# One tile's look-ahead and two ring slots fewer in a routed expert stage, and weight splitting moved from VectorE to GpSimd

## The reference

```python
def _moe(x, gate, w1, w2, w3):              # x: 4096 tokens of 256
    probs = softmax(xf @ gate)              # 4 experts
    w, idx = top_k(probs, 2); w = w / sum(w)
    comb = einsum('nk,nke->ne', w, one_hot(idx, 4))
    for e in range(4):
        h = silu(xf @ w1[e]) * (xf @ w3[e])           # 256 -> 768
        out = out + comb[:, e:e+1] * (h @ w2[e])      # 768 -> 256
...
x = x + _moe(_rmsnorm(x, g2), gate, w1, w2, w3)
...
x = x + s * silu(x_ffn)                     # the end of layer 1
```

## Time and profile before

| | |
|---|---|
| device time, median of 3 | 3390.69 us (3389.99 to 3396.9) |
| profiled execution | 3396.9 us, of which the span from first to last instruction is 3395.1 |
| busy in the span | TensorE 3159.0 us, VectorE 2242.8, ScalarE 2053.3, GpSimd 1165.1 |
| mean granted TensorE clock | 0.963 |
| routing stage | from 2769.4 to 2872.5 us |
| expert stage | from 2872.5 us to the end |

### The profile page before, as it was taken

How to read it: one execution, slowest core, us unless ns; L and a number is a source line. 1 busy time by engine, 2 the same in 40 slices (tenths; PEclk the granted TensorE clock), 3 DMA queues, 4 the chain that set the end, 5 groups by cost and what they waited for, 6 DMA issues and landing times. The chain is left out here.

```text
span 3395.1 us, 75760 instructions
## 1 busy us (share of the span) xinstructions
PE 3159.0 (93%) x23170; PEld 2407.6 (71%) x23170; DVE 2242.8 (66%) x6696; ACT 2053.3 (60%) x4941; POOL 1165.1 (34%) x1836
## 2 busy tenths in 40 slices
PE   4999999999999999999999988969999974999995
PEld 3777776777767767668888865546666664999995
DVE  5888888888888888876566655556666626333334
ACT  4777777777777777765655543226656644333433
POOL 4444444444444444443333320043242202333331
PEclk9999999999999999999999998969999976999998
DMA  3111111111111111143333431010111133223225
GB/s 87 34 36 36 33 28 31 36 36 36 36 32 36 36 36 36 32 144 125 131 111 129 136 124 50 32 49 25 34 44 33 33 107 113 35 39 88 37 37 169
DMA packets 143913, 208.80 MB, mean 62 GB/s; under 512 B 29762, under 2 KB 101826, under 8 KB 143778
## 3 DMA queue, kind: packets, MB, share of 16 engines
q1 hardware_dynamic: 130914, 189.46, 18.7%
q0 software_dynamic: 12864, 17.57, 3.2%
HBM read 123.22 MB, written 39.98 MB: 48 GB/s over the span
## 5 line engine op out<-in xcount | busy, mean ns | idle before, releaser
L770 POOL TENSOR_SCALAR at_p<-at_p,at_recip 128x512 f32<-128x512 f32 (+3 forms) x1030 | 538.1, 539 | 824.6 <-DVE at_recip L917 824.6
L826 ACT ACTIVATE at_p<-at_p,at_nmax 128x512 f32<-128x512 f32 (+3 forms) x1032 | 571.5, 556 | 130.4 <-DVE at_nmax L911 124.0
L911 DVE CUSTOM_DVE_ANT_0 at_p<-at_s_ps,at_bias 128x512 f32<-128x512 f32 (+3 forms) x1032 | 462.2, 488 | 63.3 <-PE at_s_ps L1043 44.7
L1889 DVE CUSTOM_DVE_ANT_0 aa_a_ps<-aa_a_ps,aa_hidden 128x128 f32<-128x128 f32 (+3 forms) x512 | 247.3, 507 | 177.1 <-PE aa_a_ps L2053 174.0
L1043 PE MATMUL at_s_ps<-at_k_twice,at_q 64*128 64x512 f32 (+3 forms) x3096 | 342.2, 340 | 3.1 <-DVE at_nmax L911 3.1
L1065 PE MATMUL at_o_ps<-at_pT,at_v 128*64 128x512 f32 (+3 forms) x2064 | 307.7, 440 | 0.0
L1789 ACT ACTIVATE aa_pT<-aa_b_ps 128x512 f32<-128x512 f32 (+1 forms) x384 | 196.7, 529 | 180.6 <-PE aa_b_ps L2071 177.9
L923 DVE COPY at_pT<-at_t_ps 128x512 f32<-128x512 f32 (+3 forms) x512 | 239.2, 488 | 94.0 <-PE at_t_ps L1055 90.2
L1055 PEld LDWEIGHTS at_t_ps<-ident,at_p 64*128 64x128 f32 x5120 | 189.2, 138 | 120.5 <-issue 120.5
L449 ACT ACTIVATE nw_h<-nw_h_ps,nw_b 128x512 f32<-128x512 f32 x192 | 132.3, 689 | 210.6 <-PE nw_h_ps L553 210.1
L526 DVE SCALAR_TENSOR_TENSOR nw_hl<-nw_h,nw_coef_now,nw_hh 128x512 fp32r<-128x512 f32 x192 | 150.2, 782 | 163.8 <-ACT nw_hh L454 163.8
(11 more groups left out here) (307 smaller groups left out, 7807.3 us busy)
## 6 DMA issues: line engine op xcount, KB each, us to landing
at_k_twice<-at_k_twice SPq DMA_DIRECT2D x130, 256.0 KB, 2.8
nw_w_raw<-in_w_all_dram SPq DMA_DIRECT2D x26, 1024.0 KB, 5.0
nw_w_raw<-in_w_all_dram SPq DMA_DIRECT2D x52, 512.0 KB, 6.8
w_all<-in_w_dram SPq DMA_DIRECT2D x12, 768.0 KB, 10.1
nw_xh<-xh_dram SPq DMA_DIRECT2D x10, 512.0 KB, 4.2
nw_xl<-xl_dram SPq DMA_DIRECT2D x10, 512.0 KB, 4.8
at_w_raw<-in_w_heads_dram SPq DMA_DIRECT2D x18, 256.0 KB, 3.7
nw_x<-in_x_dram SPq DMA_DIRECT2D x9, 512.0 KB, 6.0
```

What stands on the lines that cost most here:

```text
L770: pool.tensor_scalar(p, p, recip[:, u:u + 1], 1.0, ALU.mult, ALU.mult).then_inc(scaled, 1)
L826: act.activation(p_sb[:, u, 0:N], p_sb[:, u, 0:N], ACT.Exp, bias=nmax[:, u:u + 1], scale=-1.0, accum_out=total[:, u:u + 1]).then_inc(exped, 1)
L911: dve.tensor_tensor_reduce(out=p_sb[:, u, 0:N], in0=s_ps[u % 2][:, score_at(u // 2)], in1=bias[:, u % 2, S - N:S], scale=1.0, scalar=BIG, ...
L1889: dve.tensor_tensor_reduce(out=a_ps[i % 2][:, 0:N], in0=a_ps[i % 2][:, 0:N], in1=hidden[:, S - N:S], scale=1.0, scalar=BIG, op0=ALU.add, o ...
```

## The change

The expert stage keeps 3 buffers of gathered rows in place of 5, and turns the rows of tile t + 1 in unit 2t, right ahead of its hidden sums, in place of in unit 2t - 1; `take_x` and `rest_x` move with it. In routing the splitting during the votes is gone. ScalarE sums the squares of a batch before it copies the turned batch, and makes all 24 high parts behind the norms. GpSimd makes the 12 low parts of experts 2 and 3: six before the first part of the list, and two after each of the first three parts. VectorE makes those of experts 0 and 1 after `places`, as before.

```diff
-XRING = 5
+XRING = 3
...
-        SPLITS = [(e, piece) for e in (2, 3, 0, 1) for piece in W_PIECES]
-        SPLIT_BY = [0, 0, 0, 0, 2, 4, 6, 9, 12]
...
@@ routing_phase, gpsimd @@
+            def split_low(number, e, piece):
+                hi, lo = (slice(at, at + W_PIECE) for at in W_PIECES[piece])
+                pool.wait_ge(w_high, number + 1)
+                pool.tensor_tensor(w_all[:, e, lo], w_all[:, e, lo].bitcast(F32), w_all[:, e, hi].bitcast(F32), ALU.subtract)\
+                    .then_inc(w_low, 1)
+
             pool.memset(blank[:], 0.0).then_inc(blanked, 1)
             pool.wait_ge(loaded, 48)
+            pieces = [(e, piece) for e in (2, 3) for piece in range(len(W_PIECES))]
+            for number in range(6):
+                split_low(number, *pieces[number])
+
             for j in range(PARTS):
                 pool.wait_ge(marked, 2 * j + 2)
                 pool.tensor_tensor(told[j % 2][:, :, 0, :], in_tile[j % 2][:],
...
+                if j < PARTS - 1:
+                    for number in (6 + 2 * j, 7 + 2 * j):
+                        split_low(number, *pieces[number])
...
@@ routing_phase, scalar @@
             for b in range(B):
+                square(b)
                 copy_turned(b)
-                square(b)
-                for number in range(SPLIT_BY[b], SPLIT_BY[b + 1]):
-                    split_high(number)
...
             for b in range(2, B):
                 norm(b)
-            for number in range(SPLIT_BY[B], len(SPLITS)):
-                split_high(number)
+            for e in (2, 3, 0, 1):
+                act.wait_ge(w_loaded[e], 48)
+                for hi, lo in W_PIECES:
+                    act.activation(w_all[:, e, hi:hi + W_PIECE], w_all[:, e, lo:lo + W_PIECE].bitcast(F32), ACT.Copy)\
+                        .then_inc(w_high, 1)
...
@@ routing_phase, vector: in the votes @@
-                if b > 0:
-                    for number in range(SPLIT_BY[b - 1], SPLIT_BY[b]):
-                        split_low(number)
-            for number in range(SPLIT_BY[B - 1], SPLIT_BY[B]):
-                split_low(number)
...
@@ expert_phase, scalar (vector alike, with rest_x) @@
             take_x(0)
             pass_gate(0)
-            take_x(1)
...
-                if half == 1 and t + 2 < TILES:
-                    take_x(t + 2)
+                if half == 0 and t + 1 < TILES:
+                    take_x(t + 1)
...
@@ expert_phase, tensor @@
             turn_x(0)
             hidden_sums(0)
-            turn_x(1)
             hidden_sums(1)
             turn_hidden(0)
             for U in range(UNITS):
                 t, half = divmod(U, 2)
                 if half == 0 and t + 1 < TILES:
                     whose(t + 1)
-                if half == 1 and t + 2 < TILES:
-                    turn_x(t + 2)
+                    turn_x(t + 1)
                 if U + 2 < UNITS:
                     hidden_sums(U + 2)
```

More of the change, by code:

```diff
@@ L2383, in _ @@
             dve.wait_ge(loaded, 48)
[L2385 to L2389, removed]
             for k in range(KT):
@@ L2512, in _ @@
             dve.tensor_copy(shares[:], list_ps[:, LANES:2 * LANES]).then_inc(placed, 1)
-            for number in range(SPLIT_BY[B], len(SPLITS)):
-                split_low(number)
+            number = 2 * len(W_PIECES)
+            for e in (0, 1):
+                for hi, lo in (tuple(slice(at, at + W_PIECE) for at in piece) for piece in W_PIECES):
+                    number += 1
+                    dve.wait_ge(w_high, number)
+                    dve.tensor_tensor(w_all[:, e, lo], w_all[:, e, lo].bitcast(F32), w_all[:, e, hi].bitcast(F32), ALU.subtract)\
+                        .then_inc(w_low, 1)
         @block.tensor
@@ L2702, in _ @@
             gate(0)
-            rest_x(1)
             for U in range(UNITS):
@@ L2710, in _ @@
                     .then_inc(h_low, 1)
-                if half == 1 and t + 2 < TILES:
-                    rest_x(t + 2)
+                if half == 0 and t + 1 < TILES:
+                    rest_x(t + 1)
             for b in range(B):
```

## The result

The changed kernel takes 3609.13 us (median; 3603.01 to 3609.13, 3 runs) against 3390.69: the ratio is 1.0633, interval 1.0607 to 1.0658. It is slower, and lies beyond the forecast's range, which ended at 3600. Its profiled execution took 3604.48 us with a span of 3602.7, 207.6 more than the span of before; the mean granted clock went from 0.963 to 0.948. The forecast's sum was +159, and it is made against spans, so 48.6 us are to be explained.

What follows compares the result with a forecast made beforehand. The prediction took TensorE to bound the expert stage and VectorE's chain to set routing's end. Stall 141.2, ring +2, backlog -2 and routing +18 made +159 us: 3556 profiled, 3550 against the median, range 3512 to 3600.

Steps and rivals of the forecast that it cites:

- I take it that the clock holds, narrowly: Expert stage: TensorE keeps its full clock despite a pause of 2.16 us in 9.3.
- a clock of 0.5 in the expert stage: Expert stage: one of three signs in the profile after that would show the forecast wrong.
- Rival (b): Expert stage: the clock falls after some or all pauses, costing 33 to 88 us, 3583 to 3638; chance 0.17.
- The stall, 2.14 a tile: Expert stage: TensorE waits for the turned rows' round trip at half 0 of tiles 1 to 66, 141.2 us.
- Rival (d): Expert stage: shorter round trip, take_out and hh not in front, 1.60 a tile, 106 + 18: 3515; chance 0.08.
- The ring of three, +2: Expert stage: gathered rows come 0.8 late at the two places with side loads, with spill 2 us in all.
- Rival (f): Expert stage: ring too short throughout, each tile 0.8 longer if every gather took 7.3 us, +53: 3603; chance 0.03.
- The backlog at the tail, -2: End of expert stage: the last scatter's 2.91 us hold by earlier ones is gone with longer tiles, -2 us.
- Routing, +18: Routing stage: VectorE and GpSimd take turns; 5.4 before the first told, 10.7 between them, 2 for half clock.
- Rival (c): Routing stage: VectorE and GpSimd do not shut each other out, 141 - 3 = +138, 3529; chance 0.10.

Runs made afterwards that it cites:

- filler runs: Changed kernel with 1, 2, 3, 4 or 12 extra products of 128 columns, results unused, in the pause: 3603.84, 3606.03, 3606.42, 3556.95, 3556.40 us.
- e4: Changed kernel with take_x ahead of take_out and hh on ScalarE, and rest_x ahead of hl on VectorE: 3526.35 us, ratio 1.039.
- e3: Kernel before with only the changed routing stage, ring and order of the expert stage as before: 3405.49 us, ratio 1.0039.
- e7: Kernel with the routing part alone, but all 24 low parts on VectorE behind the list and none on GpSimd: 3400.81 us, ratio 1.0026.

## Why the prediction was wrong, by its own steps

- **"I take it that the clock holds, narrowly": this step failed.** The clock fell after 34 of the 66 pauses, at 1.56 us each, 53 us. The prediction had named a clock of 0.5 in the expert stage as a sign of being wrong, and it is there. The filler runs show that it is the clock and that the pauses cause it: the same tile at the same 9.41 us, with 34 falls or with two. Whether the pauses in the attention stage fall for the same reason was not tried. The prediction discounted the pauses of 1.83 us in the earlier trace rows because thin work stands around them; wide work around the pause did not hold the clock at 1.98, 1.80 or 1.69 us. The Trainium skill ("TensorE: Matmul & The Clock Gate", section "HAM oscillation — how this bites in real kernels") tells of a kernel whose clock fell at every group of products, behind waits of some 3 to 5 us. The pauses here are shorter, 1.98 us, and the clock fell at nearly every second one, which that kernel does not show. Rival (b) carried this case with 0.17 and its interval, 3583 to 3638, holds the result. Its share of tiles (a quarter to two thirds) fits 34 of 66; its price of 2 us a tile was 1.56; its condition, "from a pause a little longer than mine on", was wrong, as 1.69 was enough.
- **The stall, 2.14 a tile.** The mechanism held, and each station within 0.05 us: `take_out`, `hh`, `take_x` at +0.19, +0.57 and +0.94 after the turn's start, `rest_x` ended at +2.21, TensorE on at +2.35. The sum took the wrong start for today: it had TensorE go on at E + 0.24, the whole cost of the transpose, but in the kernel before the hidden sums begin 0.13 after the turn (3059.02 - 3058.89):

```profile
3059.02 0.96 PE L2746 MATMUL ex_a_ps<-w_all,ex_xh 128*128 x4
```

  The other 0.1 of the 0.24 is that these four products, right behind a turn, take 0.96 where they take 0.85 elsewhere, and that is paid in both orders (2924.38 has 0.96 too). So the stall is 2.35 - 0.13 = 2.22, or 2.23 by the period: 147.2 in place of 141.2. Rival (d), with `take_x` in front, was refuted by ScalarE's timeline; e4 shows what it would have been.
- **The ring of three, +2.** It did not show: in the changed kernel TensorE never waits for `xg`. Where the clock holds (four extra products) the wait comes, in exactly the two places named, 1.34 and 2.10 us, 3.4 in all. Longer tiles give the gather more time, but that they hid the wait was only argued: with three extra products and as many long tiles there is one wait of 1.79 us. Rival (f) was refuted: median landing stays 2.8 us.
- **The backlog at the tail, -2.** The tail is 1.6 shorter, for about the reason given, though the wait that it named is still there. GpSimd's last two scatters, before and after:

```profile
3359.49 1.55 POOL L2638 DMA_INDIRECT moe_dram<-ex_o,places  x1 [5.21 <-DMA moe_dram<-ex_o,places]
...
3567.18 1.57 POOL L2637 DMA_INDIRECT moe_dram<-ex_o,places  x1 [7.84 <-ACT ex_o L2655]
3571.77 1.55 POOL L2637 DMA_INDIRECT moe_dram<-ex_o,places  x1 [3.02 <-DMA moe_dram<-ex_o,places]
```

  The last scatter is held for 3.02 by the one before it, as it was for 2.91. But that one is no longer late: it waited for ScalarE and not for an older scatter. The last one begins 1.4 us after the last output sums (3570.4) in place of 2.7 (3361.2 to 3363.95).
- **Routing, +18.** It was +13.1 here, measured against the block's own start, and +15.0 in the routing part alone (e3). The Exp's wait went from 3.82 to 0.44, the 3.4 forecast. One subtraction takes 1.81 (10.85 / 6), 1.8 forecast, while it is VectorE that is held. The first `told` is 2.2 later and not 5.4: the first subtraction began 1.8 earlier than I had it, and the six ended at 2829.67. Of VectorE's six steps drawn out beside them, all of which the forecast had at 1.8, three took that and the others 1.36, 1.27 and 0.86. The 1.8 by which the first began earlier are chance, by the earlier end of the voting; in e3, where the voting ends as late as before, the first `told` is 4.1 later. The `told` stand 9.56 apart (forecast 10.0), 9.4 in place of 10.7. Between them two subtractions take 6.66, so there GpSimd is held as well, which the forecast's 1.8 each left out. The last listing products are slower by 1.66 (2 forecast). Rival (c), no shutting out, is refuted by e3 and e7: twelve subtractions on GpSimd take the `told` from 6.4 to 9.6 apart, and without them they stand at 6.4.
- **Forecast against median.** The profiled execution of before lay 6.2 above its median and that of after 4.65 below its own; this makes 10.9 of the 59 us between 3550 and 3609.13. The other 48.6 are +53 (clock), +6 (stall), -5 (routing), -2.9 (before routing), -2 (ring), and -0.5 of smaller rests.

## What to carry to other kernels

When an edit puts a pause of some 2 us into each pass of a loop that TensorE bounds, cost it twice: as the idle time, and as the half clock that follows it, which added 53 us to the 147 of the idle time here. If the trace holds even a few pauses shorter than yours after which the clock fell, take that as the likeliest case. And look-ahead in the order of work and look-ahead in buffers are worth what the other one leaves: three buffers cost 6% in one order and nothing that shows in the other.

## What the runs showed of the hardware

- With pauses of 1.98, 1.91, 1.80 and 1.69 us in a tile of 9.41 us the clock fell in 33 to 35 of 66 tiles, in near strict turns: a tile at half the clock for its hidden sums, and then one at the full. With 1.58 it fell only beside a wait for `xg` in the profiled execution, though another execution was 10 us slower at a lower mean clock. These are kernels of one shape; what exactly the chip weighs is not shown by them.
- Filling the pause with four products that nobody reads made the changed kernel 52 us faster (3609.13 to 3556.95).
- While GpSimd subtracts, VectorE's `rt_run` of two inputs (L2467) takes 1.81 us in place of 0.29 for the same step in the kernel before and in e7, and `rt_slot_u` L2477, of one input, 1.27, where it takes 0.20 in those two; the reduces of the same stretch stay at 0.38. The Trainium skill ("SBUF — State Buffer", section "Who interferes with whom") says that a two-input operation contends with GpSimd's reads and that a reduce never does, and the trace agrees. The one-input step is another case, and no run here tells why it waited.
- The four products right behind a turn of rows take 0.96 us, without a pause (3059.02 in the kernel before) and with one of 1.98 (2924.38), where the same four take 0.85 or 0.86 elsewhere. Their ends are modelled, but from start to start it is 0.80 against 0.70 in both traces. The cost comes with the turn and not with the pause.
